# New orders for every engine of a DLRM interaction kernel, and its pads zeroed half by GpSimd, half by VectorE

## What is computed

```python
e = jnp.stack([tbl_0[ids[:, 0]], ..., tbl_25[ids[:, 25]]], axis=1)
all_emb = jnp.concatenate([bottom_output[:, None, :], e], axis=1)
gram = jnp.einsum('bfd,bgd->bfg', all_emb, all_emb)
z = gram[:, _TRIU_I, _TRIU_J]
h = jnp.concatenate([z, r_bottom_output], axis=1)
h = jnp.maximum(h @ W_top1 + b_top1, 0.0)
h = jnp.maximum(h @ W_top2 + b_top2, 0.0)
y = h @ W_top3
```

## Time and profile before

| what | us |
|---|---|
| median of three runs | 130.43 |
| profiled execution | 132.01 |
| its span, first instruction to last | 130.2 |
| TensorE busy | 110.0 |
| GpSimd busy | 71.5 |
| VectorE busy | 61.7 |
| ScalarE busy | 53.2 |

### The profile page before, as it was taken

How to read it: one execution, slowest core, us unless ns; L and a number is a source line. 1 busy time by engine, 2 the same in 40 slices (tenths; PEclk the granted TensorE clock), 3 DMA queues, 4 the chain that set the end, 5 groups by cost and what they waited for, 6 DMA issues and landing times.

```text
span 130.2 us, 1962 instructions
## 1 busy us (share of the span) xinstructions
PE 110.0 (85%) x702; PEld 98.4 (76%) x702; DVE 61.7 (47%) x145; ACT 53.2 (41%) x97; POOL 71.5 (55%) x78
## 2 busy tenths in 40 slices
PE   0399999999999799899305899539999999999993
PEld 0178878887888588799305699539999999999892
DVE  5799999969999980042002220033203332542220
ACT  4466694199684523353002254041232273342021
POOL 4787787877877887747877087727272000007000
PEclk9999999999999999999955558965799999999999
DMA  4998959825999211211212221202211001102000
GB/s 89 244 237 203 253 181 248 214 57 165 250 310 272 66 43 45 60 40 40 60 47 66 56 58 40 60 23 69 65 47 45 0 0 33 29 3 53 7 0 1
DMA packets 7481, 12.31 MB, mean 95 GB/s; under 512 B 3420, under 2 KB 4356, under 8 KB 7472
## 3 DMA queue, kind: packets, MB, share of 16 engines
q1 hardware_dynamic: 5200, 7.78, 22.7%
q0 software_dynamic: 2208, 4.36, 13.0%
q10 hardware_dynamic: 64, 0.07, 0.2%
HBM read 11.40 MB, written 0.00 MB: 88 GB/s over the span
## 4 chain that ended last, share of the span: by engine, by line
PE 46%; POOL 21%; another core or an unknown queue 11%; issue 8%; DMA 6%; ACT 5%; DVE 0%; ACTq 0%
POOL feat L329 21%; PE psG L417 19%; PE psL L445 8%; PE psL L459 6%; DMA feat<-in_tbl,idx 5%; PE psX L375 3%; PE psX L376 3%; PE psL L435 3%; ACT z L533 3%; PE psX L390 2%; ACT featT L510 2%; DMA idx<-in_ids 2%; PE psL L467 1%; PE psG L390 0%
## 5 line engine op out<-in xcount | busy, mean ns | idle before, releaser
L329 POOL DMA_INDIRECT feat<-in_tbl,idx x64 | 67.4, 1053 | 30.0 <-issue 17.4
L417 PE MATMUL psG<-featT 128*123 128x108 f32 x256 | 34.1, 296 | 7.6 <-ACT z L533 6.6
L417 PEld LDWEIGHTS psG<-featT 128*123 128x123 f32 x256 | 32.8, 211 | 8.7 <-ACT z L533 7.6
L375 PE MATMUL psX<-onehot,hi 125*128 125x512 f32 x82 | 33.5, 409 | 0.2 <-issue 0.2
L376 PE MATMUL psX<-onehot,lo 125*128 125x512 f32 x82 | 33.0, 402 | 0.0
L599 DVE TENSOR_SCALAR onehot<-ids_rel 125x512 fp32r<-125x512 f32 x82 | 29.5, 430 | 0.3 <-ACT ids_rel L527 0.3
L605 DVE COPY z<-psG 27x216 f32<-27x216 f32 x32 | 12.2, 383 | 29.5 <-remote 16.5
L510 ACT ACTIVATE featT<-psX 128x512 f32<-128x512 f32 (+2 forms) x21 | 17.1, 830 | 15.0 <-PE psX L376 13.9
L533 ACT ACTIVATE z<-psG 27x216 f32<-27x216 f32 x32 | 10.8, 339 | 29.2 <-PE psG L417 16.1
L375 PEld LDWEIGHTS psX<-onehot,hi 125*128 125x128 f32 x82 | 16.0, 195 | 4.5 <-issue 1.3
L376 PEld LDWEIGHTS psX<-onehot,lo 125*128 125x128 f32 x82 | 16.0, 196 | 3.2
(11 more groups left out here) (31 smaller groups left out, 56.8 us busy)
## 6 DMA issues: line engine op xcount, KB each, us to landing
whole<-in_tbl SPq DMA_DIRECT2D x8, 448.0 KB
feat<-in_tbl,idx POOLq DMA_INDIRECT x64, 2.6
w1z<-in_w_pairs SPq DMA_DIRECT2D x1, 768.0 KB
whole<-in_tbl SPq DMA_DIRECT2D x1, 560.0 KB
w<-in_W SPq DMA_DIRECT2D x1, 512.0 KB
whole<-in_tbl SPq DMA_DIRECT2D x2, 224.0 KB
whole<-in_tbl SPq DMA_DIRECT2D x8, 52.0 KB
bottomT<-in_bottom_t SPq DMA_DIRECT2D x1, 256.0 KB
```

Of the source, the lines that this page charges most:

```text
L329: nc.gpsimd.indirect_dma_start(feat[:, k % FU, i, :], None, tables[f - 1], bass.IndirectOffsetOnAxis(idx[:, t, f - 1:f], 0)).then_inc(rows ...
L375: nc.tensor.matmul(out, hi[:, q % PB, r, :], onehot[:, c % RV, :], start=(r == 0), stop=False)
L417: done = nc.tensor.matmul(psG[n % 2][0:FS * (GS - 1) + F, g // GB, (g % GB) * GS * F:(g % GB + 1) * GS * F], later, four[:, :, 0:F], start ...
```

## The change

The four strings are written anew. In TensorE's, t6 stands before the last lookup s9, t9 and t10 stand together before g6, t11 comes behind a2, and grams alternate otherwise with layers 1 to 3. ScalarE, VectorE and SyncE get strings that fit it. The second part of the last table's copy has a letter of its own (f) and stands behind z0. The pads of tiles 0 and 1 are zeroed by GpSimd, those of tiles 2 and 3 by VectorE, which now makes ident_r before it clears ids_rows. The layers are written for batches of tiles (`BATCHES`), of which each holds one tile, so their instructions have the same shapes as before.

```diff
+    BATCHES = [(0,), (1,), (2,), (3,)]
...
-    ZEROED_P = 1
+    ZEROED_P = 2
...
-    PE_PLAN = steps("""i0 i1 i2 s0 i3 s1 t0 i4 i5 s2 i6 t1 s3 s4 i7 t2 s5 i8 t3 s6 s7 t4 i9 t5 s8 s9 g0 t6 g1 t7 g2 t8 g3
-        g4 g5 t9 g6 t10 g7 a0 a1 t11 a2 a3 g8 t12 g9 b0 b1 t13 g10 c0 a4 g11 a5 a6 t14 a7 t15 b2 t16 b3 g12
-        g13 g14 g15 c1 a8 a9 a10 a11 b4 b5 c2 a12 a13 a14 a15 b6 b7 c3""")
+    PE_PLAN = steps("""i0 i1 i2 s0 s1 i3 t0 i4 i5 s2 i6 s3 i7 t1 t2 s4 t3 i8 s5 s6 t4 i9 s7 t5 s8 t6 s9 g0 t7 g1 g2 t8 g3
+        g4 g5 t9 t10 g6 a0 a1 a2 t11 g7 a3 b0 t12 g8 b1 t13 g9 c0 g10 a4 a5 g11 t14 a6 t15 a7 t16 b2 g12 b3
+        g13 c1 g14 g15 a8 a9 a10 a11 b4 b5 c2 a12 a13 a14 a15 b6 b7 c3""")
...
-    SP_PLAN = steps("""w0 w1 w2 w3 w4 k w5 w6 w7 w8 w9 m p0 p1 p2 p3""")
+    SP_PLAN = steps("""w0 w1 w2 w3 w4 w5 w6 k w7 w8 w9 m p0 p1 p2 p3""")
...
-                    if former == ("e", LK - 1):
-                        rest = ("e", LK)
+                    if former == ("e", HALVED):
+                        rest = ("f", 0)
...
-                out = psL[bank][:, o // 2, :]
-                nc.tensor.matmul(out, w1b[:, P * o:P * (o + 1)], bottomT[:, P * t:P * (t + 1)],
-                                 start=True, stop=False)
+                out = layer_out(bank, k, o // 2)
+                nc.tensor.matmul(out, w1b[:, P * o:P * (o + 1)], bottomT[:, cols], start=True, stop=False)
...
+            dve.wait_ge(ident_made, 1)
+            nc.vector.tensor_copy(ident_r[:], ident[:]).then_inc(ident_r_made, 1)
             nc.vector.memset(ids_rows[2 * HEAD:P // 2], 0).then_inc(ids_zeroed, 1)
             nc.vector.memset(ids_rows[P // 2:P], 0).then_inc(ids_zeroed, 1)
-            dve.wait_ge(ident_made, 1)
-            nc.vector.tensor_copy(ident_r[:], ident[:]).then_inc(ident_r_made, 1)
             nc.vector.memset(featT[:, ZEROED_P:TILES, :, :, F:FS], 0.0).then_inc(pads_zeroed_v, 1)
```

More of the change, by code:

```diff
@@ L98, in dlrm_program, with samples_of @@
     last = TILES - 1
+    BATCHES = [(0,), (1,), (2,), (3,)]
+    WIDEST = max(len(tiles) for tiles in BATCHES)
+    def samples_of(n):
+        tiles = BATCHES[n]
+        return slice(P * tiles[0], P * (tiles[-1] + 1)), P * len(tiles)
     CH = 3
@@ L394, in tile_written @@
                 needed = [("y", k) for k in range(len(units)) if units[k][0] == t] + [("k", 0)]
-                needed += [("e", q) for q in range(LK if t == 0 else LK + 1)]
+                needed += [("e", q) for q in range(LK)] + [("f", 0)] * (t > 0)
                 for engine in ("act", "dve"):
@@ L424, in layer_1 @@
             def layer_1(n):
-                t, o = divmod(n, N1)
+                k, o = divmod(n, N1)
+                tiles = BATCHES[k]
+                cols, _ = samples_of(k)
                 if n == 0:
@@ L449, in layer_2, with layer_3 @@
             def layer_2(n):
-                t, o = divmod(n, N2)
-                first, second = (h1_a, h1_v) if t % 2 == 0 else (h1_v, h1_a)
+                k, o = divmod(n, N2)
+                _, width = samples_of(k)
+                first, second = (h1_a, h1_v) if k % 2 == 0 else (h1_v, h1_a)
                 if o == 0:
-                    pe.wait_ge(first, 2 * (t + 1))
+                    pe.wait_ge(first, 2 * (k + 1))
                 for c in range(N1):
                     if (o, c) == (0, 1):
-                        pe.wait_ge(second, 2 * t + 1)
+                        pe.wait_ge(second, 2 * k + 1)
                     elif (o, c) == (0, N1 - 1):
-                        pe.wait_ge(second, 2 * (t + 1))
-                    done = nc.tensor.matmul(psL[(o + t) % 2][:, 2, :], w2[:, c, P * o:P * (o + 1)],
-                                            h1[:, c, :], start=(c == 0), stop=(c == N1 - 1))
+                        pe.wait_ge(second, 2 * (k + 1))
+                    done = nc.tensor.matmul(layer_out((o + k) % 2, k, 0), w2[:, c, P * o:P * (o + 1)],
+                                            h1[:, c, 0:width], start=(c == 0), stop=(c == N1 - 1))
                 done.then_inc(l2_done, 1)
-            def layer_3(t):
+            def layer_3(k):
+                _, width = samples_of(k)
                 for c in range(N2):
-                    pe.wait_ge(h2_made[(c + t) % 2], t + 1)
-                    done = nc.tensor.matmul(psL[t % 2][:, 3, :], w3[:, c:c + 1].to_broadcast([P, P]), h2[:, c, :],
-                                            start=(c == 0), stop=(c == N2 - 1))
+                    pe.wait_ge(h2_made[(c + k) % 2], k + 1)
+                    done = nc.tensor.matmul(layer_out(k % 2, k, 1), w3[:, c:c + 1].to_broadcast([P, P]),
+                                            h2[:, c, 0:width], start=(c == 0), stop=(c == N2 - 1))
                 done.then_inc(l3_done, 1)
@@ L572, in _ @@
                     copy_table(act, act_copy, n).then_inc(fcopied_a, 1)
+                elif kind == "f":
+                    copy_table(act, act_copy, HALVED, rest=True).then_inc(fcopied_a, 1)
                 elif kind == "y":
```

106 lines of the change are left out of this document (59 added, 47 removed).

## The result

The changed kernel takes 138.69 us (median of 4 runs, 136.06 to 141.37) against 130.73 for the kernel before on the same chip (4 runs, 129.18 to 132.66). The ratio is 1.053 with a 95% interval of 1.027 to 1.079: slower. It compares the quicker executions of each kernel (136.06 and 138.09 against 129.18 to 131.03), since some of either kernel run a few per cent longer. The forecast was 127.4, with a range of 121 to 133, so the time lies outside it and the sign was wrong. The profiled execution is the quickest, 136.06 us with a span of 134.3. Against before's 132.01 us and 130.2 it is 4.05 us longer, and it is this difference that the rows can tell of.

What follows compares the result with a forecast made beforehand. Taken as the bound: TensorE's rests and half clock between 63 and 93 us, from late rises. Terms -0.9 and -3.1 gave -4.0; -3 was taken, so 129.0 us profiled, 127.4 median, range 121 to 133.

Steps and rivals of the forecast that it cites:

- What bounds the kernel: 63 to 93 us: 6.6 + 3.6 us of TensorE silence and some 7.5 at half clock, from late rises while GpSimd gathers.
- the change's premise: Whole kernel: TensorE's semaphore rises queue behind its own matmul records; the forecast doubted this, citing the skill.
- come out when either rests: TensorE's rises pile up after 2 us or so of short matmuls beside gathers, and are released when TensorE or GpSimd rests.
- Start: Kernel start, pads' memsets and identity copy: 0, between -0.4 us (VectorE ready earlier) and +0.5 (a shared delay).
- Lookups: Lookups, 7 to 52 us: 0, between -1.0 (a gather wait goes) and +1.5 (VectorE feeds a matmul late).
- t6 before s9: Before the last lookup: first gram at 53.3, z0 copied at 61.4, TensorE rests nearly 5 us, g2 at 62.1.
- To t9 and t10: From g2 on: g5 through at 73.1, t9 and t10 together end at 74.0, GpSimd restarts 0.7 us sooner.
- Layer 1 of tile 0: First layer-1 groups: packs land at about 79.2, TensorE waits 3.3 us before a0, and the clock may fall again.
- Sum: Whole kernel: -0.9 (a2 done) - 3.1 (full clock after 87) = -4.0; from -4 to -2, -3 taken.
- full clock after 87: From 87 us on TensorE runs at full clock where before had half until 93.1; worth -3.1 us.
- Tail: Last stretch, same TensorE-bound matmuls with b0, a3 and c0 moved among grams: 0, between -0.5 and +1.5.
- The stall only moves forward: Rival, slower: rises stay held while first grams run, g5 ends at 77.6, +3.9 us, 134.3 or 132.4; chance 0.20.

Runs made afterwards that it cites:

- the wide row: Kernel after with 40 matmuls of 512 columns, reading only the identity, put behind unit 7's transpose and before the first gram block; 143.0 us in one run.

## Why the prediction was wrong

*What bounds the kernel.* The reading was right in the late rises and their link with GpSimd's gathers, and so was the doubt about the change's premise. "NOTIFIC — the notification-queue block" in the Trainium skill, section "10. Constraints, capacities, measured rates", states that emitting an implicit record costs the engine no cycles. The runs without gathers and with plain loads agree: the same 702 matmul records, no rise late. The clause "come out when either rests" holds in part: z0 came at 60.43, 1.6 us into TensorE's rest, with gathers going on to 61.75; but in before the copy at 68.77 came 5.7 us into one. That it takes short matmuls was wrong: the wide row is held too.

*Start.* Booked at 0, between -0.4 and +0.5; it cost 1.04 in the trace and 1.0 to 1.2 in a run of its own. I counted the shrunk memset and the moved cast, and gave the cast no longer time for standing beside GpSimd's memset. The row shows it at 1.38 us, ending 0.09 us after the memset. The Trainium skill's page "SBUF — State Buffer", section "SBUF: two separate sides", speaks of a port pair that VectorE and GpSimd hold one at a time; this case's rows agree, 1.38 us beside and 0.23 when the memset was all but over.

*Lookups.* Booked at 0, between -1.0 and +1.5; they lost 0.39 (1.87 at the first gram, less 1.04 and less the 0.44 of t6, which the forecast had there too). Within the bounds.

*t6 before s9.* The times were near: z0 at 60.43 for a foretold 61.4, TensorE's rest 2.52 us for nearly 5, g2 at 61.37 for 62.1. The step between them was not: I had GpSimd's next halt let z0's rise out, and z0 was copied 1.3 us before that halt began (61.75). So the nearness is in part luck.

*To t9 and t10.* Foretold was g5 through at 73.1 and both units done at 74.0, since "at half clock the rise of g5 was not far off". g5 began at 72.32, and unit 10's transpose at 77.32: the rise of g3 (ended 68.5) was held to 71.38, that of g4 (70.2) to 75.93, and ScalarE's copy of unit 8 stands behind that one. That 0.7 us sooner for GpSimd became 1.6 later (76.39 against 74.83).

*Layer 1 of tile 0.* "So TensorE waits 3.3 us before a0 and the clock may fall once more" is what the kernel does where no rise is held: 3.12 us and a fall. I had the loss on paper and set it against the 3.6 us of silence in before, as if the one took the other's place for nothing. In the profiled kernel with gathers it didn't appear, as TensorE came to a0 late, at 80.95.

*Sum.* The -4.0, of which I took -3, stood: between the first gram and 93.25 the kernel won 4.0 on before. Not all of its parts did: "full clock after 87" held from 81.4 to 98.4 only, and the stalls at 72 and 77 weren't foretold. So that the two numbers agree so closely is chance.

*Tail: the step that failed.* "0, between -0.5 and +1.5" came out as +6.7. The kernel was 2.6 us ahead at 93.25 and 4.1 behind at the end: 4.5 lost up to 99.93, in stops of 3.4 us and slow matmuls between them, and 2.2 more at half clock behind it. b1, t13, g9 and c0 now stood where GpSimd makes seven gathers in a row, and the stall that I had taken for past came again. I had read the dense, prompt rises from 93.1 on the earlier trace rows as a property of the place in the program; but in before GpSimd halts there for 2.59 and for 1.07 us between its last gathers, and from 99.5 on it has none to make:

```profile
94.06 0.94 POOL L329 DMA_INDIRECT feat<-in_tbl,idx  x1 [2.59 <-PE psX L390]
...
98.57 0.94 POOL L329 DMA_INDIRECT feat<-in_tbl,idx  x1 [1.07 <-PE psX L390]
```

With the start (1.04) and the lookups (0.39): -4.0 + 1.4 + 6.7 = +4.1.

*What no term held.* With no rise held at all, new orders and start still cost 4.5 to 4.7 us, by the wait for the packs and the clock behind it. The forecast had no term for what the orders cost by themselves.

*The rivals.* "The stall only moves forward" was the nearest: right in its sign, and the stall did move. Its condition, GpSimd catching g1's rise again, was met for g3 and g4, but its place was wrong: g5 began at 72.3 and not later than 74, and at 93 the kernel was ahead of before. That its price (+3.9) is close to the profiled +4.05 is luck. It should have had more than 0.20: a stall tied to an engine that has 30 of its 64 gathers still to make when the grams begin can't be planned away at one place.

What remains open: why one chip of the five held no rises (one batch ran on it, so the chip and the occasion aren't told apart); whether any of this happens in an execution that isn't recorded, since every one here has its recorded span and clock; and whether the stops inside TensorE's blocks are a queue that has filled. The page "NOTIFIC — the notification-queue block" of the Trainium skill, section "7.1 Overflow: three behaviours, one of which stalls the engine", says that the block's inner pipeline makes its producers wait and doesn't drop records. A stop with nothing awaited, after 3.8 us of short matmuls but 9.7 us of mostly wide ones, would look like that; no run here counts what fills it.

## What to carry to other kernels

Where rises come late, take away the suspected partner altogether before planning around it: one run without half of the gathers told in one number (0.88) what no reading of orders could. A forecast for a hand-made order should ask where the other engine's long runs of work will stand under the new order, not only what happens at the place that was mended. And compare orders in a kernel with the disturbance taken out too: new orders and start cost 4.5 us by themselves, about 1 of it the start, which the disturbance had hidden from view.
